# Second experts: the places of a tile's rows are copied into a small ring before the tile's results are sent

## The chip, the cores and the metric

The kernel runs on one core of a Trainium2 chip. The metric is the device time of one execution in microseconds (us), and the median over several runs is compared. The core has five engines that work side by side: TensorE (PE in the profile, its weight loads PEld), VectorE (DVE), ScalarE (ACT), GpSimd (POOL) and SyncE (SP), which here only starts transfers. The engines meet through semaphores.

## The reference

Two layers over x of 32 x 128 tokens with 128 channels. Each layer is an attention and then a mixture of experts, in which every token goes to 2 of 8 experts. The second mixture, which the change touches, is this for each chosen expert, and a shared expert on top for every token:

```
def _expert(x, w1, b1, w3, b3, w2, b2):
    h = jax.nn.silu((x @ w1 + b1) * (x @ w3 + b3))
    return h @ w2 + b2
...
biased = scores + gate_b
_, idx = lax.top_k(biased, K)
w = jnp.take_along_axis(scores, idx, axis=-1) * ROUTER_SCALE
```

D is 128, the hidden width 176, E is 8 and K is 2. The results of the two chosen experts are weighted by w and added.

## The kernel before, in words

Attention writes each token's row twice into a DRAM tensor `rows`, sorted by expert. A row has 132 numbers: the token's normed values, its place (column `IDX`, the row of `results` to which the expert's result belongs) and its weight (column `WGT`). The experts then work on tiles of 128 such rows. There are at most SLOTS = 71 tiles in a layer, and which expert a tile belongs to is read at run time from a map.

For a tile i of the second experts (`gated_experts`) the steps are:

- SyncE loads it into `xs`, slot i % 16 (`load`, L1884). XU = 16 slots form the ring.
- TensorE transposes it (`take`, L2045), ScalarE copies the transpose out (L1942), and TensorE multiplies by the expert's first weights (`widen`, L2059), which VectorE has copied from the resident weights (L1982).
- ScalarE and VectorE form the product and the SiLU (L1948, L1989, L1957), and TensorE multiplies by the second weights (`narrow`, L2078).
- VectorE scales the result by the rows' weights, read from `xs`, into `ys`, slot i % 8 (L2001). U = 8 slots form that ring, and VectorE waits until the send of tile i - 8 has landed.
- GpSimd sends the 128 result rows to their places in the DRAM tensor `results` by an indirect transfer (`send`, L1929). Before the change it reads the places straight from the tile in `xs`.

The tiles go in pairs: one unit of work holds two routed tiles or two rows of blocks for the shared expert. The list UNITS starts with 7 shared units, then come 36 routed ones with three shared ones between, and 6 shared ones stand at the end. Of a unit u, TensorE does the first product, then takes the tiles of unit u + 2, then does the second product of unit u - 2.

Since the places are in `xs`, a slot of `xs` may be loaded anew only when the send that reads it has landed. So `load(i)` for i of 16 and more waits for the transpose (L1880), the scaled result (L1881) and the landed send (L1882) of tile i - 16. SyncE handles all its transfers in program order. Behind the last of the 71 loads stands `combine`: SyncE waits until the first 55, then 63, then all 71 sends have landed (`results_stored`, L1893), and after each loads a piece of the combined results into `yg` (L1901, named first_w in the trace). These are added by VectorE or, for the last blocks, by TensorE (L2084), the blocks 28 to 31 last.

The first experts (`experts`) already have the form with a copied place: `note` (L1618) copies it on GpSimd to `xi` with 8 slots, `send` (L1625) reads it there. There the note of tile n + 1 stands before the send of tile n. `early` in the trace is the memory that holds `ys`.

Of the kernel before, what the change touches and what calls it, by code (L numbers as in the profile page):

```python
# [14 lines left out]
U32 = mybir.dt.uint32  # L15
ALU = mybir.AluOpType
# [19 lines left out]
SLOTS = 2 * N // 128 + E - 1  # L36
# [4 lines left out]
X0, IDX, WGT = 1, D + 1, D + 2  # L41
# [194 lines left out]
class Steps:  # L236
# [10 lines left out]
    def wait(self, eng):  # L247
        eng.wait_ge(self.sem, self.n)
# [6 lines left out]
def attention(nc, st, layer, w):  # L255
# [156 lines left out]
    def fill_up(eng, experts):  # L412


        eng.wait_ge(st["maps_ready"], layer + 1)
        for e in experts:
            count = 128 * (1 if e < E - 1 else 1 + PAST)
            first = nc.s_assert_within(eng.value_load(st["fill"][0:1, e:e + 1]), 0, (e + 1) * REGION - 128,
                                       skip_runtime_bounds_check_because="a region has room for all the tokens")
            eng.dma_start(rows[bass.ds(first, count), :], st["filling"][e * 128:e * 128 + count, :]).then_inc(filled, 16)  # L420
# [1114 lines left out]
def experts(nc, st, w, maps_set, early_set):  # L1535

    U = 8
    FC = 4
    ctx, sh = st["ctx"], st["shared"]

    def sem(name):
        return ctx.enter_context(nc.semaphore(f"{name}_e0"))
# [4 lines left out]
    xs, xi, xsT, ys, w1s = sh["xs"], sh["xi"], sh["xsT"], sh["ys"], sh["w1s"]  # L1547
# [3 lines left out]
    hTp, xTp, yp = banks[0:2], banks[2][:, 0, :], banks[3][:, 0, :]  # L1551

    xs_in = st["xs_in"]
    xi_copied = sem("xi_copied")
    xsT_ready, xsT_copied = sem("xsT_ready"), sem("xsT_copied")
    hT_ready, hT_copied = sem("hT_ready"), sem("hT_copied")
    yp_ready, ys_ready = sem("yp_ready"), sem("ys_ready")
    ys_out = st["ys_out"][0]
    w1_copied = st["w1_copied"] = sem("w1_copied")
    rows, results = w["rows"], w["results"]  # L1560
# [202 lines left out]
def gated_experts(nc, st, w, early_set, maps_set, x_updated, shared_turned):  # L1763
# [7 lines left out]
    U = 8  # L1771
    XU = 16
# [4 lines left out]
    ctx, sh = st["ctx"], st["shared"]  # L1777

    def sem(name):
        return ctx.enter_context(nc.semaphore(f"{name}_e1"))  # L1780
# [1 line left out]
    x, cst, emap, rowmap = st["x"], st["cst"], st["emap"], st["rowmap"]  # L1782
    ident = cst[:, C_ID:C_ID + 128]
    W1r, W1s, W2, bsh = st["W1r"], st["W1s"], w["W2"], st["bsh"]
    xs, ys, yg, xall = sh["xs"], sh["ys"], sh["yg"], st["xall"]
    xsT, cs, hm, hT, w1s = sh["xsT2"], sh["cs"], sh["hm"], sh["hT2"], sh["w1s2"]
    S, ptp = sh["S"], sh["ptp"]

# [3 lines left out]
    w1_copied = sem("w1_copied")  # L1792
    up_ready, cs_ready, hm_ready, hT_ready = sem("up_ready"), sem("cs_ready"), sem("hm_ready"), sem("hT_ready")
    yp_ready, ys_ready, z_ready = sem("yp_ready"), sem("ys_ready"), sem("z_ready")
    ys_out = st["ys_out"][1]
    results_in = [sem(f"results_in{c}") for c in range(4)] + [st["pairs_in"]]
    landed = [32] * 4 + [32 * (NP // 2) + 32]
    x_done, dve_step = sem("x_done"), sem("dve_step")
    rows, results = w["rows"], w["results"]
# [69 lines left out]
    def row_of(eng, i):  # L1869
        return nc.s_assert_within(eng.value_load(mapped(rowmap, i, EARLY)), 0, SHARED - 128,  # L1870
                                  skip_runtime_bounds_check_because="the map's rows are those of its experts' tiles")
# [4 lines left out]
    def load(sp, i, row=None):  # L1876

        s, before = i % XU, i - XU
        if i >= XU:
            sp.wait_ge(xsT_ready, before // 2 + 1)  # L1880
            sp.wait_ge(ys_ready, before + 1)  # L1881
            sp.wait_ge(ys_out[before % U], 16 * (before // U) + 16)  # L1882
        at = row_of(sp, i) if row is None else row
        sp.dma_start(xs[:, s, :], rows[bass.ds(at, 128), :]).then_inc(xs_in[s], 16)  # L1884

    def in_place(eng, i):

        eng.wait_ge(xs_in[i % XU], first_use[i % XU] + 16 * (i // XU) + 16)
# [32 lines left out]

    def gpsimd(pool):

        def send(i):

            s, place = i % U, xs[:, i % XU, IDX:IDX + 1].bitcast(U32)
            in_place(pool, i)
            pool.wait_ge(ys_ready, i + 1)
            nc.gpsimd.indirect_dma_start(results[:, :], bass.IndirectOffsetOnAxis(place, 0), ys[:, s, :], None).then_inc(ys_out[s], 16)  # L1929

        for i in range(SLOTS):
            send(i)

    def scalar(act):
# [101 lines left out]
    def tensor(pe):  # L2036
# [51 lines left out]
        for u in range(NU + 2):  # L2088
# [17 lines left out]
            yield u  # L2106

    return {"load": load, "first_row": first_row, "combine": combine, "gpsimd": gpsimd, "scalar": scalar,
            "vector": vector, "tensor": tensor}


def build(nc, dram):

    with ExitStack() as ctx:
# [67 lines left out]
        prefetch += [(st["W1r"][:, :, :], dram["e1_W1"]), (st["W1s"][:, :], dram["e1_sW1"]), (st["bsh"][:, :], dram["e1_sB"]),  # L2182
                     (w1["W2"][:, :, :, :], dram["e1_W2"])]
        for name in ("cst_in", "three_set", "consts_in", "ident_ready", "weights_in", "maps_ready", "x_out", "bias_in", "raw_in", "stats_ready",
                     "w1_less"):
            st[name] = ctx.enter_context(nc.semaphore(f"{name}_all"))
        st["xs_in"] = [ctx.enter_context(nc.semaphore(f"xs_in{s}_all")) for s in range(8)]
        st["lasts_in"] = [ctx.enter_context(nc.semaphore(f"lasts_in{i}_all")) for i in range(2)]
# [5 lines left out]
        results = [nc.dram_tensor(f"results{l}", (2 * N + (E + PAST) * 128, D), F32, kind="Internal").ap() for l in range(2)]  # L2194
# [3 lines left out]
        def later_loads(sp):  # L2198

            sp.dma_start(st["cst"][:, C_SOON:], dram["cst"][:, C_SOON:]).then_inc(st["consts_in"], 16)  # L2200
            for l in range(2):
# [7 lines left out]
        a0 = attention(nc, st, 0, {**{k: dram[f"a0_{k}"] for k in names + ("am", "amT", "pad", "padT")},  # L2209
                                   "rows": rows[0], "prefetch": prefetch, "last_weights": last_weights})  # L2210
        e0 = experts(nc, st, {**w0, "rows": rows[0], "results": results[0]}, a0["maps_set"], a0["early_set"])
        a1 = attention(nc, st, 1, {**{k: dram[f"a1_{k}"] for k in names}, "gb": dram["e1_gb"], "rows": rows[1],
                                   "results": results[0], "prefetch": []})
        e1 = gated_experts(nc, st, {**w1, "rows": rows[1], "results": results[1]}, a1["early_set"], a1["maps_set"], a1["x_updated"], a1["shared_turned"])

        def run(part):
# [175 lines left out]
```

## Time and profile before

| | |
|---|---|
| median of 3 runs | 696.37 us (694.57 to 697.83) |
| span of the profiled execution | 763.9 us |
| profiled span less the median | 67.5 us |
| TensorE busy | 671.5 us, 88% |
| VectorE busy | 523.5 us, 69% |
| GpSimd busy | 504.9 us, 66% |
| ScalarE busy | 415.8 us, 54% |

The rows of the trace come from one execution under the hardware profiler. Its span is longer than the runs that give the median. In a row of a timeline the first number is the start, the second how long the merged instructions last, and what stands in brackets is the idle time of the engine before them with what ended it. "issue" means that nothing in the profile ended it.

### The profile page before, as it was taken

To read this page: it belongs to the slowest core of one execution; us is meant where nothing else is said; L and a number is where in the kernel's file an instruction comes from. 1 tells how busy PE (TensorE), PEld (TensorE's weight loads), DVE (VectorE), ACT (ScalarE), POOL (GpSimd) and SP (SyncE) were. 2 spreads that over 40 slices of the span, in tenths; PEclk is the share of its full clock that TensorE was granted. 3 is DMA by queue.
4 is the path that set the end of the run, shared out by engine and by line. 5 is a ranking of instruction groups with operands and counts; after the bars stand their busy time and mean duration, and the time that the engine had idled before them with its cause. 6 is when DMAs were issued, how large, how long until landed. Compare 5 with 4: busy or idle time off the path is not lost.

```text
span 763.9 us, 21054 instructions
## 1 busy us (share of the span) xinstructions
PE 671.5 (88%) x7092; PEld 546.5 (72%) x7092; DVE 523.5 (69%) x1515; ACT 415.8 (54%) x1158; POOL 504.9 (66%) x837
## 2 busy tenths in 40 slices
PE   8799998888876999999979999888888668788797
PEld 7567666665646999999957776666667568778787
DVE  5489988888663446555358898888886555555556
ACT  5477767654542434444447777656547445555563
POOL 5975788577564678877677778777667635455451
PEclk9899999999997999999979999999989989899999
DMA  5470000001331522343110101111211312222264
GB/s 166 124 305 2 17 27 27 27 30 36 137 99 48 160 70 81 97 127 89 46 36 29 30 26 40 54 37 37 66 34 37 89 51 77 61 75 72 75 232 152
DMA packets 45406, 57.78 MB, mean 76 GB/s; under 512 B 11379, under 2 KB 37142, under 8 KB 44630
## 3 DMA queue, kind: packets, MB, share of 16 engines
q1 hardware_dynamic: 36086, 38.17, 16.6%
q0 software_dynamic: 8640, 17.97, 7.1%
q8 instruction: 60, 0.98, 0.5%
q10 hardware_dynamic: 576, 0.29, 0.1%
q14 instruction: 44, 0.36, 0.1%
HBM read 33.82 MB, written 22.08 MB: 73 GB/s over the span
## 4 chain that ended last, share of the span: by engine, by line
PE 50%; POOL 17%; issue 12%; DVE 8%; ACT 5%; another core or an unknown queue 4%; DMA 2%; SPq 1%; DVEq 0%; POOLq 0%; ACTq 0%
POOL results L1625 9%; PE ptp L1349 8%; PE M L1366 7%; PE ptp L2078 6%; PE S L1326 5%; PE S L2059 5%; PE S L1330 3%; PE ptp L1352 3%; POOL xi L1618 2%; POOL rows L626 2%; PE M L1374 2%; PE M L1418 2%; PE S L2065 1%; SPq L707 1%
## 5 line engine op out<-in xcount | busy, mean ns | idle before, releaser
L626 POOL DMA_INDIRECT rows<-out_rows,posi x128 | 126.9, 991 | 50.1 <-issue 32.1
L806 ACT ACTIVATE pT<-ptp 128x512 f32<-128x512 f32 (+1 forms) x192 | 95.1, 525 | 97.7 <-PE ptp L1349 87.0
L1929 POOL DMA_INDIRECT results<-early,xs x71 | 69.0, 971 | 68.4 <-DVE early L2001 50.9
L1064 DVE TENSOR_REDUCE mx<-S 128x16 f32<-128x1232 f32 x64 | 91.3, 1427 | 18.3 <-PE S L1330 16.4
L1625 POOL DMA_INDIRECT results<-early,xi x71 | 75.9, 1069 | 40.5 <-DVE early L1687 35.1
L1065 DVE TENSOR_TENSOR pr<-S,mx 128x1232 f32<-128x1232 f32 x64 | 92.3, 1442 | 2.2
L1724 PE MATMUL S<-first_w,early 128*128 x568 | 77.2, 279 | 3.0 <-DVE early L1687 1.5
L1714 PE MATMUL S<-early,w1s 128*128 128x128 f32 x568 | 76.9, 279 | 0.6 <-ACT early L1659 0.6
L1366 PE MATMUL M<-pT,vm 128*32 128x128 f32 (+1 forms) x2048 | 74.7, 283 | 1.1 <-ACT pT L806 0.6
L1349 PE MATMUL ptp<-cst,pr 128*128 128x128 f32 x512 | 74.0, 290 | 0.0
L1724 PEld LDWEIGHTS S<-first_w,early 128*128 128x128 f32 x568 | 69.5, 193 | 5.9 <-issue 5.7
L1687 DVE TENSOR_SCALAR early<-S,xs 128x128 f32<-128x128 f32 x71 | 24.9, 351 | 68.0 <-PE S L1724 39.2
L1714 PEld LDWEIGHTS S<-early,w1s 128*128 128x128 f32 x568 | 70.8, 196 | 0.9 <-ACT early L1659 0.9
L1349 PEld LDWEIGHTS ptp<-cst,pr 128*128 128x128 f32 x512 | 58.6, 147 | 16.1 <-issue 16.0
L1659 ACT ACTIVATE early<-S 128x128 f32<-128x128 f32 x71 | 19.7, 277 | 90.3 <-PE S L1707 51.7
L2078 PE MATMUL ptp<-W,kT 128*128 (+1 forms) x412 | 63.6, 301 | 5.4 <-ACT kT L1959 3.8
L1366 PEld LDWEIGHTS M<-pT,vm 128*32 128x32 f32 (+1 forms) x2048 | 52.5, 112 | 18.1 <-issue 13.8
L2078 PEld LDWEIGHTS ptp<-W,kT 128*128 128x128 f32 x412 | 57.4, 212 | 8.8 <-issue 7.8
L2059 PE MATMUL S<-early,w1s 128*128 128x128 f32 x426 | 60.2, 297 | 3.1 <-issue 1.3
L2059 PEld LDWEIGHTS S<-early,w1s 128*128 128x128 f32 x426 | 57.1, 213 | 4.1 <-issue 4.0
L1326 PE MATMUL S<-first_w,qT 32*128 32x308 f32 x512 | 52.5, 479 | 6.9 <-POOL first_w L569 2.8
L1989 DVE TENSOR_TENSOR pr<-S,pr 128x256 f32<-128x256 f32 (+1 forms) x72 | 26.7, 413 | 41.7 <-ACT pr L1948 24.4
(221 smaller groups left out, 1527.9 us busy)
## 6 DMA issues: line engine op xcount, KB each, us to landing
xs<-rows SPq DMA_DIRECT2D x142, 66.0 KB
first_w<-in_e_W SPq DMA_DIRECT2D x2, 2048.0 KB, 8.2
swap<-results SPq DMA_DIRECT2D x32, 128.0 KB
first_w<-results SPq DMA_DIRECT2D x6, 512.0 KB
rows<-out_rows,posi POOLq DMA_INDIRECT x128
x_res<-in_x SPq DMA_DIRECT2D x1, 1536.0 KB, 8.4
W1r<-in_e_W SPq DMA_DIRECT2D x1, 1536.0 KB, 10.8
out_x<-x_res SPq DMA_DIRECT2D x3, 512.0 KB, 2.7
```

The lines of the kernel that those rows point to most:

```text
L626: nc.gpsimd.indirect_dma_start(rows[:, :], bass.IndirectOffsetOnAxis(posi[:, k, n:n + 1], 0), out_rows[:, ring_slot(groups, n), k, :], Non ...
L806: nc.scalar.activation(pT[0:rows_of, G * r:G * r + count, :], ptp[q % 2][0:rows_of, 0:count, :], ACT.Exp, scale=SCALE)\
L1064: do(V.tensor_reduce(mx[:, :].rearrange("p (g j) -> p g j", g=G), sc, AX.X, ALU.max))
L1065: V.tensor_tensor(pr[:, n % 2, :, :].rearrange("p (g j) k -> p g j k", g=G), sc, mx[:, :].rearrange("p (g j) -> p g j", g=G).unsqueeze(3). ...
L1326: nc.tensor.matmul(S[:, g, 0:GK], qT[heads, n % 2, :], kexp[heads, n % KR, :, :], start=True, stop=True, skip_group_check=True)
L1349: last = nc.tensor.transpose(ptp[q % 2][:, g, :], flat[:, g // 2, at:at + 128], ident)
L1366: last = nc.tensor.matmul(OT[32 * g:32 * g + 32, half * T:(half + 1) * T], vm[0:rows_of, n % 2, block + g, :], pT[0:rows_of, chunk, :], st ...
L1625: nc.gpsimd.indirect_dma_start(results[:, :], bass.IndirectOffsetOnAxis(xi[:, s:s + 1], 0), ys[:, s, :], None)\
L1714: last = nc.tensor.matmul(hTp[n % 2][:, c, :], w1s[:, n % 3, c * 128:(c + 1) * 128], xsT[:, n % 3, :], start=True, stop=True)
L1724: last = nc.tensor.matmul(yp, hT[:, n % 2, c, :], w2[:, c, :], start=(c == 0), stop=(c == FC - 1))
L2059: last = nc.tensor.matmul(out[:, at * 128:(at + 1) * 128], w1s[:, u % 2, at, c * 128:(c + 1) * 128], xsT[:, r % 3, at, :], start=True, sto ...
L2078: last = nc.tensor.matmul(yp(u)[:, at, :], hT[:, u % 2, c * 256 + at * 128:c * 256 + (at + 1) * 128], w2[:, c, :], start=(c == 0), stop=(c ...
```

## The change

The second experts get a `note` of their own. It copies the places of tile i to `xi`, slot i % 8, right before the send of tile i, and the send reads them there. The load of tile i then waits for the copied place of tile i - 16 in the place of its landed send. The semaphore `xi_copied` is shared by both layers, so the second starts its count at SLOTS.

```
-            sp.wait_ge(ys_out[before % U], 16 * (before // U) + 16)
+            sp.wait_ge(xi_copied, SLOTS + before + 1)
...
     def gpsimd(pool):
 
+        def note(i):
+
+            s = i % U
+            wait(pool, ys_out[s], 16 * (i // U))
+            in_place(pool, i)
+            nc.gpsimd.tensor_tensor(xi[:, s:s + 1], xs[:, i % XU, IDX:IDX + 1].bitcast(U32), st["zero"][:, 0:1], ALU.add).then_inc(xi_copied, 1)
+
         def send(i):
 
-            s, place = i % U, xs[:, i % XU, IDX:IDX + 1].bitcast(U32)
-            in_place(pool, i)
+            s = i % U
             pool.wait_ge(ys_ready, i + 1)
-            nc.gpsimd.indirect_dma_start(results[:, :], bass.IndirectOffsetOnAxis(place, 0), ys[:, s, :], None).then_inc(ys_out[s], 16)
+            pool.wait_ge(xi_copied, SLOTS + i + 1)
+            nc.gpsimd.indirect_dma_start(results[:, :], bass.IndirectOffsetOnAxis(xi[:, s:s + 1], 0), ys[:, s, :], None)\
+                .then_inc(ys_out[s], 16)
 
         for i in range(SLOTS):
+            note(i)
             send(i)
```

## Rows read from the trace of the kernel before

**Rows 1.** Busy time by stage, from 580 us on (time, then busy us and count).

```profile
core 0: us, PE busy (x) PEld busy (x) DVE busy (x) ACT busy (x) POOL busy (x), PEclk, DMA share, GB/s
...
580.00:764.00 184.00, 148.07 (x1064) 138.28 (x1064) 107.57 (x345) 95.25 (x248) 90.34 (x97) 0.92 0.30 94
```

**Rows 2.** The chain of waits, 712 to 726 us (start, us, what).

```profile
714.85 1.34 PE S L2059 x12
...
722.21 2.02 PE S L2059 x12
```

**Rows 3.** Waits of TensorE, 612 to 764 us (total, times, longest).

```profile
PE M L2045 <- ACT early L1942: 13.9, 7, 4.6
...
PE M L2045 <- issue: 3.6, 3, 2.0
```

**Rows 4.** Waits of GpSimd, 612 to 764 us.

```profile
POOL results L1929 <- DVE early L2001: 50.9, 20, 8.3
POOL results L1929 <- issue: 17.4, 51, 1.0
```

**Rows 5.** Timeline of GpSimd, 739 to 749 us.

```profile
740.32 0.96 POOL L1929 DMA_INDIRECT results<-early,xs  x1 [2.17 <-DVE early L2001]
741.58 0.96 POOL L1929 DMA_INDIRECT results<-early,xs  x1 [0.30 <-issue]
...
747.94 0.96 POOL L1929 DMA_INDIRECT results<-early,xs  x1 [0.30 <-issue]
```

**Rows 6.** The line of the sends (duration in ns, first and last start).

```profile
L1929 POOL DMA_INDIRECT results<-early,xs x71: 956/962/1217, 619.9 to 747.9; - x71
```

**Rows 7.** Timeline of SyncE's loads, 622 to 689.6 us, and the last alone.

```profile
622.68 66.81 SPq L1884 DMA_DIRECT2D xs<-rows  x36
...
689.15 0.33 SPq L1884 DMA_DIRECT2D xs<-rows  x1
```

**Rows 8.** Timeline of SyncE, 749.5 to 751.5 us.

```profile
750.34 0.80 SPq L1901 DMA_DIRECT2D first_w<-results  x2
```

**Rows 9.** Timeline of VectorE, the last scaled result.

```profile
744.60 0.33 DVE L2001 TENSOR_SCALAR early<-ptp,xs 128x128 f32<-128x128 f32 x1
```

**Rows 10.** The line of TensorE's takings up to 695.3 us.

```profile
L2045 PE MATMUL M<-cst,xs x52: 272/273/475, 600.8 to 695.2; 128*128 128x128 f32 x52
```

**Rows 11.** Transfers by issue (KB each, median us to landing).

```profile
out_x<-x_res SPq DMA_DIRECT2D x2, 256.0 KB, 2.7
...
bv<-in_a_bv ACTq DMA_DIRECT2D x1, 64.0 KB, 3.7
```

**Rows 12.** Waits of SyncE, 618 to 764 us.

```profile
SPq L1893 <- DMA results<-early,xs: 11.6, 3, 9.8
SPq L1882 <- DMA results<-early,xs: 8.0, 15, 1.7
```

**Rows 13.** Timeline of GpSimd in the first experts, 353 to 358 us.

```profile
353.47 1.05 POOL L1625 DMA_INDIRECT results<-early,xi  x1 [0.45 <-DVE early L1687]
354.55 0.20 POOL L1618 TENSOR_TENSOR xi<-xs,zero 128x1 uint32<-128x1 uint32 x1
354.91 1.22 POOL L1625 DMA_INDIRECT results<-early,xi  x1 [0.16 <-POOL xi L1618]
...
356.52 0.99 POOL L1625 DMA_INDIRECT results<-early,xi  x1 [0.16 <-POOL xi L1618]
```

**Rows 14.** Timelines of GpSimd and VectorE in the first experts, 309 us.

```profile
309.11 0.44 POOL L1618 TENSOR_TENSOR xi<-xs,zero 128x1 uint32<-128x1 uint32 x1
...
309.09 0.42 DVE L1680 COPY w1s<-first_w 128x512 f32 x1
```

**Rows 15.** Timeline of TensorE, 756.3 to 760 us.

```profile
757.08 0.61 PE L2084 MATMUL ptp<-first_w,cst 128*128 128x128 f32 x4
```

**Rows 16.** Timeline of ScalarE, 742 to 751 us.

```profile
750.42 0.42 ACT L1957 ACTIVATE kT<-pr 128x256 f32<-128x256 f32 x1 [3.40 <-remote]
```

More of the change, by code:

```diff
@@ L1553, in experts @@
     xs_in = st["xs_in"]
-    xi_copied = sem("xi_copied")
+    xi_copied = st["xi_copied"]
     xsT_ready, xsT_copied = sem("xsT_ready"), sem("xsT_copied")
@@ L1784, in gated_experts @@
     W1r, W1s, W2, bsh = st["W1r"], st["W1s"], w["W2"], st["bsh"]
-    xs, ys, yg, xall = sh["xs"], sh["ys"], sh["yg"], st["xall"]
+    xs, ys, xi, yg, xall = sh["xs"], sh["ys"], sh["xi"], sh["yg"], st["xall"]
     xsT, cs, hm, hT, w1s = sh["xsT2"], sh["cs"], sh["hm"], sh["hT2"], sh["w1s2"]
@@ L1794, in gated_experts @@
     yp_ready, ys_ready, z_ready = sem("yp_ready"), sem("ys_ready"), sem("z_ready")
-    ys_out = st["ys_out"][1]
+    ys_out, xi_copied = st["ys_out"][1], st["xi_copied"]
     results_in = [sem(f"results_in{c}") for c in range(4)] + [st["pairs_in"]]
@@ L2184, in build @@
         for name in ("cst_in", "three_set", "consts_in", "ident_ready", "weights_in", "maps_ready", "x_out", "bias_in", "raw_in", "stats_ready",
-                     "w1_less"):
+                     "w1_less", "xi_copied"):
             st[name] = ctx.enter_context(nc.semaphore(f"{name}_all"))
```

## The prediction

> **What bounds the kernel now.** I read the busy times by stage first. From 580 us to the end, the stage the change touches, TensorE works 148.07 of 184.00 us and GpSimd 90.34 [rows 1]. So TensorE carries the stage and GpSimd is second. The chain of waits says how the carrier walks. In an undisturbed stretch the products of one pair of tiles start at 714.85 us and those three pairs on at 722.21 [rows 2]: 7.36 / 3 = 2.45 us a pair, with nothing but TensorE's lines between. That is TensorE's pace, two tiles each 2.45 us.
>
> Next I asked who waits for whom. The longest wait of TensorE's taking of a tile (L2045) is for ScalarE's copy, 13.9 us in all, and the next, 3.6 us, waits for nothing the profile shows [rows 3]. Not one wait of TensorE is for a landed load. GpSimd waits for a result of VectorE in 20 cases, 50.9 us; in the other 51 it has its next tile already and only pays its own gap [rows 4].
>
> GpSimd's own pace comes from its timeline. Where results are ready, sends start at 740.32, 741.58, ... 747.94, seven of them: 7.62 / 6 = 1.27 us a tile, 0.96 of work and 0.30 of gap [rows 5]. A pair costs 2.54 us, already slightly more than TensorE's 2.45. It keeps up because TensorE is often slower: the 71 sends lie between 619.9 and 747.9 us [rows 6], so about 129 us with the last one's work, and need 71 x 1.27 = 90.
>
> **The change, part by part.** *1. The loads move forward.* Now the load of tile i waits for the send of tile i - 16 to land; afterwards for VectorE's result of i - 16 and for its copied place, which GpSimd takes before it waits for that result. The first such load leaves at 622.68 us [rows 7]; the send that it waits for started at 619.9 [rows 6], and that send's result was ready a little earlier. A send needs 2.40 us until SyncE passes the wait on it (the last starts at 747.94 [rows 5], the load behind it leaves at 750.34 [rows 8]), and before that a result waits for GpSimd: the last one is ready at 744.60 + 0.33 and sent at 747.94, 3.0 us later [rows 5, 9], and in the middle it is 0.8 to 2 us. So a load can leave about 3 us earlier. What is that worth? The 36th load of this series (tile 51) leaves at 689.15 [rows 7]; the 52nd taking starts at 695.2 [rows 10]: a lead of 6.0 us, the shortest of the 55 that I worked out in this way; most are 8 to 11. Loads of 66 KB have no landing time on the page; the nearest rows are 3.7 us for 64 KB and 2.7 us for 256 KB [rows 11]. Even at 3.7 us the shortest lead leaves 2.3 us. A load that comes earlier ends no wait of TensorE: worth 0. What hides it is the ring of 16 tiles. SyncE itself waits 8.0 us in 15 cases for landed results before loads [rows 12]; that wait goes, and SyncE then stands at the wait for the result instead. Behind the last load stand the loads of the combined results, whose own wait (11.6 us in 3 cases [rows 12]) needs the same sends to land as before, so they do not move forward either.
>
> *2. A copy is added before each send: 71.* The first experts run this same pair, so their rows price it. Back to back, sends start at 353.47, 354.91 and 356.52, with a copy of 0.20 between [rows 13]: 1.44 and 1.61 us a tile against 1.27. The parts: send 0.99 to 1.22, gap 0.02, copy 0.20, gap 0.16. Bounds: 0.96 + 0.02 + 0.20 + 0.16 = 1.34 from below; from above 1.22 + 0.02 + 0.44 + 0.16 = 1.84, with the copy of 0.44 us found at 309.11 [rows 14]. I take 1.50, between the two whole rounds seen, nearer the lower end because in the second experts the sends take 0.96 almost always by the median of [rows 6]. That adds 0.23 us a tile, 71 x 0.23 = 16.3 us of GpSimd.
>
> Does it lie on the path? Total first: 71 x 1.50 = 106.5 us in a stretch of 129: it fits. If the runs without a profile are shorter everywhere by the same share (696.37 / 763.9 = 0.912), the stretch is 117.5 us: still fits. Locally: in a fast stretch a pair costs GpSimd 3.00 us against TensorE's 2.45, so its lag grows by 0.55 a pair. VectorE needs the place of a result free 8 tiles, that is four pairs or 9.8 us, later; less 2.4 us of landing it bears a lag of 7.4. The lag now peaks near those 3.0 us, so some eight pairs at full pace without a break would be needed, and in the trace the pace breaks sooner: the fourth pair of the stretch of [rows 2] already takes 2.02 instead of 1.34 us for its products. Each send that has to wait for VectorE hides one copy wholly, since the copy stands before that wait. Worth 0 in the middle.
>
> A rule bears on the price of the copy. The row first: the copy of a place took 0.44 us at 309.11 where VectorE copied weights from 309.09 to 309.51, and 0.20 where it did not [rows 13, 14]. The Trainium skill, "SBUF — State Buffer", section "Who interferes with whom", says that a GpSimd instruction and a VectorE copy in a two-port mode exclude each other for the whole instruction, and whoever starts second waits. The trace agrees for these copies. By that rule a note that meets a weight copy costs 0.24 us more; the sum above goes by the rows.
>
> *3. The end.* Sends 64 to 70 run back to back [rows 5]. Six more rounds at +0.23 put the last at 749.3 instead of 747.94, and the last load of combined results at 751.7 instead of 750.34 [rows 8]. Its blocks, 28 on, are first read by TensorE at 757.08 [rows 15]: with the 2.7 us of the 256 KB row it has landed by 754.4, with 3.7 by 755.4. It fits, with 1.7 us or more to spare. But in between all engines stand (ScalarE 3.40 us until 750.42, by a releaser the profile cannot name [rows 16]). If the runs without a profile lack that stop, the slack before the change is -0.3 to 0.7 us, and the 1.4 us that the change adds cost 0.7 to 1.4. So the end costs 0 to 1.4 us, by whether that stop is there; I take 0.6.
>
> *4. The shared semaphore* counts on past the first experts' 71. It adds no wait that is not met: 0.
>
> **Sum.** Against the profiled execution: 763.9 + 0 + 0 + 0.6 = 764.5. The runs shown have a median of 696.37, 67.5 us below that span. The trace does not say where all of that lies; stops like the one in [rows 16] are a candidate. I carry the difference over unchanged: 696.37 + 0.6 = 697.0.
>
> **Rivals.** *A, GpSimd becomes the bound (slower).* The place is the 71 sends. Its point of decision: 117.5 / 71 = 1.65 us a tile. If copies meet VectorE's weight copies as at 309.11, a round is 1.50 + 0.24 = 1.74, and 71 x 1.74 = 123.5 us, 6 more than there is; with the longer lag at the end, 6 x 0.47 = 2.8 less the slack, the time is 702 to 705. For it: pairs already run at 2.54 against 2.45, and GpSimd's lag is used up fastest just where TensorE is best. Against it: only 1.44 and 1.61 were seen back to back in quiet rows, and 20 idle spells hold 50.9 us. Chance 0.17. Two or three points more go to smaller losses at the end that pass 0.5%.
>
> *B, the loads did bind (faster).* Without profiling TensorE may run closer to 2.45 us a pair throughout, and leads shrink. The ring of 16 turns 55 / 16 = 3.4 times; each turn would gain 3.2 us, less the 2.3 us of slack now seen, if that slack is truly the limit: 0.9 x 3.4 = 3; with the slack gone, 3.4 x 3.2 = 11. Time 685 to 693. For it: the profiled execution is the slower one. Against it: no wait of TensorE for a load, and slack even at 3.7 us of landing. Chance 0.13.
>
> *C, the change does not do what it says.* The copy stands behind the previous send, so if GpSimd lags, the place is copied late and the load moves less than 3 us. Nothing hangs on the move, so the time is that of my forecast, 696 to 698. It shares the chance of the forecast, together 0.68.
>
> **Numbers.** Forecast 697.0; alone it ranges from 694 to 699.5 (end cost 0 to 1.4, and the spread 694.57 to 697.83 of the runs). I stretch to 692.5, taking in the mild half of B, and to 702, where A begins. About 0.5%, 3.5 us, is what a measurement of this kernel can tell from no change. Faster by more: 0.13 (B). Within: 0.68. Slower by more: 0.19 (A and the bad ends).
>
> **What would show it.** Right: 71 new GpSimd copies of about 0.2 us; rounds of 1.44 to 1.6 us back to back; GpSimd's busy time up by 14 us or more in a stage of equal length; the first reused load leaves near 620 and leads grow by about 3 us; SyncE's 8.0 us for landed results before loads gone; still no wait of TensorE for loads. Wrong for A: VectorE's results (L2001) waiting for landed sends, sends back to back throughout, copies of 0.4 us. Wrong for B: shorter pairs in the middle, with the stretch from first to last send clearly under 129 us.

## The result, and the profile after

The change makes the kernel slower: 746.89 us (744.01 to 748.75, 4 runs) against 696.13 us (694.57 to 697.83, 4 runs), ratio 1.0711 with the 95% interval 1.0675 to 1.0748. That is 50.8 us more, against a forecast of 0.6. The profiled execution took 745.3 us with a span of 743.5, so this profile shows what the timed runs do.

Its head and its chain of waits, by engine and then by line:

```profile
span 743.5 us, 21188 instructions
...
POOL 31%; PE 24%; DVE 20%; issue 17%; DMA 4%; ACT 2%; SPq 2%; POOLq 1%; DVEq 0%; ACTq 0%
POOL results L1625 10%; POOL results L1936 7%; DVE mx L1064 5%; POOL rows L626 5%; DVE pr L1065 4%; PE ptp L1349 3%; PE M L1366 3%; PE S L1326 3%; POOL xi L1618 2%; PE ptp L2087 2%; POOL xi L1929 2%; POOL rstd L554 2%; PE S L2068 2%; PE S L1330 2%; SPq L707 1%
```

The second experts' sends and copies (now L1936 and L1929) are among the chain's lines. The line of the sends, which answers to [rows 6]:

```profile
L1936 POOL DMA_INDIRECT results<-early,xi x71: 982/985/1378, 585.2 to 728.4; - x71
...
  POOL xi L1929: 42.3, 55
...
  DVE early L2010: 13.3, 14
```

The 71 sends take 143.2 us from the first start to the last. In 55 of 71 cases the row names GpSimd's own copy as what ended the idle time. The 14 cases that name VectorE must be read with care: only the first send really waited for it. From the second send on, each send starts at least 2.40 us after its own result has ended, and the gap is 0.76 us there as well, so there too the copy was the last thing to be waited for. A stretch of GpSimd's timeline, which answers to [rows 5]:

```profile
601.50 0.98 POOL L1936 DMA_INDIRECT results<-early,xi  x1 [0.76 <-POOL xi L1929]
602.51 0.20 POOL L1929 TENSOR_TENSOR xi<-xs,zero 128x1 uint32<-128x1 uint32 x1
603.47 0.98 POOL L1936 DMA_INDIRECT results<-early,xi  x1 [0.76 <-POOL xi L1929]
604.48 0.20 POOL L1929 TENSOR_TENSOR xi<-xs,zero 128x1 uint32<-128x1 uint32 x1
605.44 0.98 POOL L1936 DMA_INDIRECT results<-early,xi  x1 [0.76 <-POOL xi L1929]
```

A round is 603.47 - 601.50 = 1.97 us: 0.98 of send, 0.03, 0.20 of copy, and 0.76 from the copy's end to the send's start. The reader should see that the copy is the small part and the gap behind it the large one. The first experts have 0.16 in that place [rows 13].

The waits of all engines, which show how the late sends pass back:

```profile
POOL results L1936 <- POOL xi L1929: 42.3, 55, 0.9
...
DVE early L2010 <- DMA results<-early,xi: 20.6, 14, 3.5
...
PE ptp L2093 <- DMA first_w<-results: 9.7, 1, 9.7
...
PE M L2054 <- DMA xs<-rows: 7.7, 12, 2.0
```

VectorE waits 20.6 us for places of the result ring to be sent. TensorE now does wait for loads, 7.7 us, since a load waits for a copy that stands behind the late sends in GpSimd's order. At the end it waits 9.7 us for the combined results. TensorE is not what carries the stage any more, although its granted clock is lower there (0.95; the kernel before has 1.00 in its second profile below): it is busy 119.78 of 147 us, in this row of the busy times by stage.

```profile
582.00:729.00 147.00, 119.78 (x879) 109.71 (x877) 86.06 (x242) 77.15 (x203) 87.09 (x143) 0.95 0.29 84
```

The waits from SyncE's side, to be held against [rows 12]:

```profile
SPq L1882 <- POOL xi L1929: 59.4, 52, 2.2
SPq L1893 <- DMA results<-early,xi: 30.7, 7, 12.2
```

So the change made the loads wait more, not less: 59.4 us for a copied place, against 8.0 us for landed sends in [rows 12] and 23.5 us in the second profile of the kernel before.

### The profile page after: what moved, and what is told of

Same layout as the page of the kernel before. It is cut to its first block, busy times and chain, and to the rows that moved or that the text cites. A ratio compares the mean times of both kernels' runs of the same rounds, so it can differ in the third digit from the quotient of the medians.

```text
span 743.5 us, 21188 instructions
## 1 busy us (share of the span) xinstructions
PE 661.2 (89%) x7092; PEld 541.9 (73%) x7092; DVE 524.1 (70%) x1515; ACT 417.7 (56%) x1158; POOL 522.9 (70%) x908
## 4 chain that ended last, share of the span: by engine, by line
POOL 31%; PE 24%; DVE 20%; issue 17%; DMA 4%; ACT 2%; SPq 2%; POOLq 1%; DVEq 0%; ACTq 0%
POOL results L1625 10%; POOL results L1936 7%; DVE mx L1064 5%; POOL rows L626 5%; DVE pr L1065 4%; PE ptp L1349 3%; PE M L1366 3%; PE S L1326 3%; POOL xi L1618 2%; PE ptp L2087 2%; POOL xi L1929 2%; POOL rstd L554 2%; PE S L2068 2%; PE S L1330 2%; SPq L707 1%
## 5 line engine op out<-in xcount | busy, mean ns | idle before, releaser
L1936 POOL DMA_INDIRECT results<-early,xi x71 | 70.9, 999 | 57.7 <-POOL xi L1929 42.3
L1625 POOL DMA_INDIRECT results<-early,xi x71 | 76.3, 1075 | 33.4 <-DVE early L1687 27.4
L1714 PE MATMUL S<-early,w1s 128*128 128x128 f32 x568 | 76.6, 279 | 0.8 <-ACT early L1659 0.8
L1349 PE MATMUL ptp<-cst,pr 128*128 128x128 f32 x512 | 72.6, 286 | 0.5 <-ACT kT L678 0.3
L1714 PEld LDWEIGHTS S<-early,w1s 128*128 128x128 f32 x568 | 70.6, 195 | 0.9 <-ACT early L1659 0.9
L1366 PE MATMUL M<-pT,vm 128*32 128x128 f32 (+1 forms) x2048 | 70.0, 277 | 0.0
L1349 PEld LDWEIGHTS ptp<-cst,pr 128*128 128x128 f32 x512 | 57.0, 144 | 16.8 <-issue 15.8
L2068 PE MATMUL S<-early,w1s 128*128 128x128 f32 x426 | 56.9, 285 | 6.9 <-DVE w1s L1991 6.5
L2068 PEld LDWEIGHTS S<-early,w1s 128*128 128x128 f32 x426 | 53.1, 200 | 8.6 <-issue 8.5
L2010 DVE TENSOR_SCALAR early<-ptp,xs 128x128 f32<-128x128 f32 x71 | 22.6, 344 | 39.0 <-DMA results<-early,xi 20.6
## 6 DMA issues: line engine op xcount, KB each, us to landing
swap<-results SPq DMA_DIRECT2D x32, 128.0 KB
```

Source lines behind the costliest of these rows:

```text
L1349: last = nc.tensor.transpose(ptp[q % 2][:, g, :], flat[:, g // 2, at:at + 128], ident)
L1366: last = nc.tensor.matmul(OT[32 * g:32 * g + 32, half * T:(half + 1) * T], vm[0:rows_of, n % 2, block + g, :], pT[0:rows_of, chunk, :], st ...
L1714: last = nc.tensor.matmul(hTp[n % 2][:, c, :], w1s[:, n % 3, c * 128:(c + 1) * 128], xsT[:, n % 3, :], start=True, stop=True)
L2068: last = nc.tensor.matmul(out[:, at * 128:(at + 1) * 128], w1s[:, u % 2, at, c * 128:(c + 1) * 128], xsT[:, r % 3, at, :], start=True, sto ...
```

## The experiments

The kernel before was timed again with each group of runs (medians 695.91 and 696.64 us), and each ratio is against the runs of its group. The last four runs below belong to the second group.

**The kernel before, once more.** Its code is unchanged. What I expected:

> The kernel before, profiled once more, because its first profile was 67.5 us longer than its timed runs while the profile of the changed kernel agrees with its own (743.5 against 745.3). Theory A (the first profile was slowed by something that the timed runs lack, and hid how tight GpSimd is): a span near 694 us, the second experts' sends within 90 to 100 us in place of 128, most of them back to back at 1.27 us, almost no rounds ended by a longer idle. Theory B (the profile is typical, the change found time elsewhere): a span near 760 again and sends over 120 us or more.

Measured: 695.13 us (8 runs), ratio 0.9997 (0.9972 to 1.0022), span 691.3. Its line of sends, its timeline of GpSimd, TensorE's only wait in this stage, SyncE's wait before loads, and the busy times by stage:

```profile
L1929 POOL DMA_INDIRECT results<-early,xs x71: 954/958/1112, 583.3 to 676.7; - x71
```

```profile
592.27 0.96 POOL L1929 DMA_INDIRECT results<-early,xs  x1 [0.30 <-issue]
593.53 0.96 POOL L1929 DMA_INDIRECT results<-early,xs  x1 [0.30 <-issue]
594.80 0.96 POOL L1929 DMA_INDIRECT results<-early,xs  x1 [0.30 <-DVE early L2001]
```

```profile
PE S L2059 <- DVE w1s L1982: 1.4, 1, 1.4
```

```profile
SPq L1882 <- DMA results<-early,xs: 23.5, 29, 2.9
```

```profile
580.00:677.00 97.00, 95.61 (x817) 94.13 (x816) 77.15 (x226) 71.56 (x192) 68.55 (x71) 1.00 0.42 126
```

The sends take 93.4 us, not the 128.0 of [rows 6]. The usual round is 1.265 us (two of them from 592.27 to 594.80), and 70 of these would be 88.6, so GpSimd has at most 4.8 us to spare in the whole stage and runs nearly without a break, beside a TensorE that is busy 95.61 of 97 us. The stops with a releaser the profile cannot name, as in [rows 16], are not there. This is what theory A said. The profile on which the prediction rests was of an execution much slower than the timed ones, and the 35 us by which its sends were spread out were taken for room.

**The copy one tile ahead.** The changed kernel, but tile i + 1 is copied before tile i is sent:

```
+        note(0)
         for i in range(SLOTS):
-            note(i)
+            if i + 1 < SLOTS:
+                note(i + 1)
             send(i)
```

> The changed kernel, with the place of tile i + 1 copied before the send of tile i, so the copy that a send waits for is one send old. Theory A (a send that waits for its own copy exposes the 0.76 us from the met wait to the start of the send, which otherwise runs under the work before): rounds of 0.98 + 0.03 + 0.20 + 0.16 = 1.37 to 1.5 us in place of 1.97, so 71 x (1.37 to 1.5 less 1.27) = 7 to 16 us over the kernel before, 703 to 713 us. Theory B (the copy itself is what costs, as work of GpSimd or by its port): no change, 740 to 750 us. Theory C (the earlier loads are in the way of the sends): 740 to 750 us too.

Measured: 704.96 us, ratio 1.0123 (1.0087 to 1.0159).

```profile
600.96 0.99 POOL L1936 DMA_INDIRECT results<-early,xi  x1 [0.16 <-POOL xi L1929]
601.97 0.20 POOL L1929 TENSOR_TENSOR xi<-xs,zero 128x1 uint32<-128x1 uint32 x1
602.33 0.99 POOL L1936 DMA_INDIRECT results<-early,xi  x1 [0.16 <-DVE early L2012]
```

The gap behind the copy is 0.16 again, a round 1.37, and 41.9 of the 50.8 us are back. The copies, loads and sends are the same; only the order differs.

**A copy that nobody reads.** The kernel before with this added ahead of a send; `unread_xi` is a tile of its own, and loads and places are as before:

```
+            nc.gpsimd.tensor_tensor(sh["unread_xi"][:, i:i + 1], st["zero"][:, 0:1], st["zero"][:, 1:2], ALU.add)
             pool.wait_ge(ys_ready, i + 1)
```

> The kernel before, with a copy of the same size on GpSimd before each send that nobody reads or waits for; loads and the source of the places as before. It computes the reference. Theory A: rounds of 1.37 to 1.5 us, 703 to 713 us. Theory B: 740 to 750 us. Theory C: no change, 696 us, but for the copy's own 0.2 us.

Measured: 701.97 us, ratio 1.0078 (1.0047 to 1.0109), a little under the range of theory A.

```profile
603.88 0.99 POOL L1930 DMA_INDIRECT results<-early,xs  x1 [0.16 <-issue]
604.90 0.20 POOL L1928 TENSOR_TENSOR unread_xi<-zero 128x1 uint32<-128x1 uint32 x1
605.25 0.99 POOL L1930 DMA_INDIRECT results<-early,xs  x1 [0.16 <-issue]
```

The copy costs 5 to 6 us by itself (3 to 8 by the interval), without any moved load. One thing more differs here: the wait for VectorE's result, an instruction of its own ahead of each send in the kernel before, is now carried by the send. What that is worth alone was not run.

**The same copy, waited for.**

```
+            ... ALU.add).then_inc(unread_set, 1)
             pool.wait_ge(ys_ready, i + 1)
+            pool.wait_ge(unread_set, SLOTS + i + 1)
```

> The same unread copy, but the send waits for it by a semaphore; loads and the source of the places as in the kernel before. Theory A: rounds of 1.97 us and the whole loss, 740 to 750 us. Theory B: the same as without the wait. Theory C: 696 to 713 us, since the loads have not moved.

Measured: 746.0 us, ratio 1.0699 (1.0662 to 1.0736): the whole loss of the change, with the source of the places and the condition of each load as before it. The difference of 44 us to the run above comes from one semaphore, which the copy raises and the next send waits for.

```profile
603.52 0.98 POOL L1933 DMA_INDIRECT results<-early,xs  x1 [0.76 <-POOL unread_xi L1930]
604.54 0.20 POOL L1930 TENSOR_TENSOR unread_xi<-zero 128x1 uint32<-128x1 uint32 x1
605.50 0.98 POOL L1933 DMA_INDIRECT results<-early,xs  x1 [0.76 <-POOL unread_xi L1930]
```

Theories B and C fall: the copy as work costs 5 to 6 us, and the loss is there without the moved loads. In the trace the wait for the copy is an instruction of its own ahead of each of the 71 sends:

```profile
L1932 POOLq EVENT_SEMAPHORE  x71: 17/17/17, 582.9 to 727.6; - x71
```

**Half of the waits.** As above, with the wait only where i is even.

> The unread copy for every tile, waited for by the sends of the even tiles alone. Theory A (each wait on the engine's own last copy costs 0.6 us of a round, by itself): rounds of 1.38 and 1.97 us in turn, 702 + 35.5 x 0.6 = 723 us, give or take 4. Rival (the waits break a flow once and for all, so half of them cost as much as all): 740 us or more; or the slack of the other rounds takes them up: under 712 us.

Measured: 724.09 us, ratio 1.0389 (1.0361 to 1.0416).

```profile
601.62 0.98 POOL L1934 DMA_INDIRECT results<-early,xs  x1 [0.16 <-DVE early L2006]
602.63 0.20 POOL L1930 TENSOR_TENSOR unread_xi<-zero 128x1 uint32<-128x1 uint32 x1
603.59 0.98 POOL L1934 DMA_INDIRECT results<-early,xs  x1 [0.76 <-DVE early L2006]
```

The gaps are 0.76 and 0.16 in turn. Each wait costs by itself, and half of them half as much: 22 of 44 us. Every copy raises the semaphore here too, so it is the wait that costs and not the raising.

**One and a half copies.** The unread, unwaited copy and a second one for every other tile.

> The unread and unwaited copy of the earlier run, and a second one for every other tile. The first copy costs only 0.11 us because it fills part of the 0.30 us gap that two sends have between them anyway; the second has no gap left. Theory A: 35.5 x 0.2 = 7 us more than the 702.0 of one copy, 707 to 711 us. Theory B (copies are hidden, and the loss of 6 us had another source): 702 us.

Measured: 708.45 us, ratio 1.0178 (1.0141 to 1.0215), 6.5 us over the single copy for 36 more copies: 0.18 us each, against 0.085 for the first (6.06 / 71, from 701.97 - 695.91). The two runs belong to different groups, whose medians of the kernel before are 0.7 us apart, so this 0.18 may be 0.16. The first copy lies in part in the 0.30 us that two sends have between them anyway:

```profile
602.15 0.20 POOL L1928 TENSOR_TENSOR unread_xi<-zero 128x1 uint32<-128x1 uint32 x1
602.30 0.20 POOL L1930 TENSOR_TENSOR unread_xi<-zero 128x1 uint32<-128x1 uint32 x1
602.65 0.98 POOL L1932 DMA_INDIRECT results<-early,xs  x1 [0.16 <-DVE early L2004]
```

**One copy for two tiles, a pair ahead.** `note` copies 128 x 2 places, and is called for i + 2 before the send of each even i.

> The changed kernel with one copy on GpSimd for the places of two tiles, a pair ahead of its sends. Theory A: half of the 0.11 us that a copy adds to a round when it stands ahead, 71 x 0.055 = 4 us over the kernel before, so about 700 us, between before and the copy ahead for every tile (705). Theory B (a copy costs by something other than the round, such as a late load): no difference from 705.

Measured: 697.14 us, ratio 1.0008 (0.9991 to 1.0025). That is cheaper than the 4 us that theory A gave.

```profile
602.61 0.98 POOL L1937 DMA_INDIRECT results<-early,xi  x1 [0.16 <-POOL xi L1930]
603.89 0.96 POOL L1937 DMA_INDIRECT results<-early,xi  x1 [0.31 <-DMA results<-early,xi]
604.88 0.20 POOL L1930 TENSOR_TENSOR xi<-xs,zero 128x2 uint32<-128x2 uint32 x1
605.24 0.98 POOL L1937 DMA_INDIRECT results<-early,xi  x1 [0.16 <-POOL xi L1930]
```

The average round is near 1.32 us, which would add 70 x 0.05 = 3.5 us, and the sends lie within 95.2 us, 1.8 more than before. So the room of up to 4.8 us seems to take up most of it; no run took that apart.

**The copy on VectorE.** The changed kernel without GpSimd's copy. VectorE makes it, before it scales the tile's result:

```
+                    V.tensor_tensor(xi[:, i % U:i % U + 1], xs[:, i % XU, IDX:IDX + 1].bitcast(U32), st["zero"][:, 0:1], ALU.add).then_inc(xi_copied, 1)
                     V.tensor_scalar(ys[:, i % U, :], yp(u)[:, at, :], xs[:, i % XU, WGT:WGT + 1], None, ALU.mult).then_inc(ys_ready, 1)
```

> The changed kernel with the copy of the place on VectorE, right before it scales the tile's result; GpSimd only sends, and the loads wait for the copied place as in the change. This is the moved load without its price on GpSimd. Theory A (GpSimd's rounds set the pace, the earlier load is worth nothing): rounds of 1.27 us again, leads of the loads 3 us longer than the 4.95 (median) of the kernel before, and the time within 0.4% of it, 694 to 699 us, with up to 3 us of loss where VectorE's 71 extra operations delay a result. Theory B (the loads were close to binding, shortest lead 2.7 us against 1.9 of landing): 5 us faster or more.

Measured: 697.53 us (12 runs), ratio 1.0024 (1.0004 to 1.0044). This is the moved load without a copy on GpSimd; VectorE has 71 copies of about 0.15 us more. GpSimd is back at its old pace:

```profile
601.63 0.96 POOL L1929 DMA_INDIRECT results<-early,xi  x1 [0.30 <-issue]
602.89 0.96 POOL L1929 DMA_INDIRECT results<-early,xi  x1 [0.30 <-DVE early L2003]
```

SyncE's waits before loads are for VectorE now, no longer for landed sends:

```profile
SPq L1882 <- DVE early L2003: 22.8, 23, 3.5
...
SPq L1882 <- DVE xi L2002: 1.0, 3, 0.4
```

From the starts of loads and takings, worked out as in the prediction, the median lead grows from 4.95 us (kernel before, second profile) to 9.1 and the shortest from 2.7 to 6.5. The time does not fall. The earlier load is had, and is worth nothing: in the second profile of the kernel before TensorE waits for no load of this stage, so there is nothing to win. No version that I ran beats the kernel before.

## Why the prediction was wrong

*The step that failed first: the gap of the copy's round.* The prediction put a round together as 0.96 + 0.02 + 0.20 + 0.16 and took 1.50 us; it measured 1.97. The 0.16 came from rows of the first experts [rows 13], where the copy of tile n + 1 stands before the send of tile n, so a send's own copy is one send old and the wait on it is met long before. In the change the copy stands right ahead of the send that waits for it. There the row that fits is another, which the prediction used only as a delay of results ("in the middle it is 0.8 to 2 us"). In the kernel before, a result that GpSimd stands idle for is sent 0.76 us after its end: the first of these two results ends at 622.48 + 0.33 = 622.81, and its send starts at 623.57.

```profile
622.48 0.59 DVE L2001 TENSOR_SCALAR early<-ptp,xs 128x128 f32<-128x128 f32 x2
...
623.57 0.96 POOL L1929 DMA_INDIRECT results<-early,xs  x1 [1.43 <-DVE early L2001]
```

There too the wait is an instruction of its own ahead of the send (71 of them at L1928). The 0.76 us belong to such a wait, not to every late wait. In the change only the wait for the copy is of that kind, and the send carries the wait for VectorE's result itself. At the first send, where the copy was long done and the result late, the gap is 0.28 us: the result started at 584.54, took 0.333 and so ended at 584.88.

```profile
585.16 1.38 POOL L1936 DMA_INDIRECT results<-early,xi  x1 [2.27 <-DVE early L2010]
```

Part 4 of the prediction has the same error in words. It says that the semaphore of the copies "adds no wait that is not met" and puts it at 0, but the send's wait on that semaphore stands right behind the copy that raises it, and was open each time: 0.60 us more a round than the 0.16 that the sum had. Even the bound from above, 1.84, was too low, since it lengthened send and copy and left the gap alone.

*The second: the room.* "71 x 1.50 = 106.5 us in a stretch of 129: it fits." The stretch is 93.4 us in an execution as long as the timed ones. The prediction saw that the profile was 67.5 us longer than the median and carried the difference over unchanged, or at best in proportion (117.5 us). By the second profile, which is 72.6 us shorter than the first, they were mostly this: the second experts' first result at 582.2 us in place of 618.8, and 34.6 us less between first and last send. Rival A had the right path, GpSimd as the bound, but not the cause: it took the copies to be longer and left the gap alone. Its point of decision, 1.65 us a round, should have been 93.4 / 70 = 1.33.

*The sum with both terms as measured:* 70 rounds at 1.97 are 137.9 us. The sends took 143.2; the other 5.3 are rounds that were longer than the usual 1.97. Less the 93.4 of before that is 49.8 us, of the 50.8 measured. Between the two profiles, 743.5 and 691.3 us long, the rest is 1.9 us by which the first send starts later and 0.5 us at the end.

*"Each send that has to wait for VectorE hides one copy wholly".* In the profile after, only the first send waited for VectorE; every later result was at least 2.40 us old when it was sent. So there was hardly any such cover.

*The end.* The prediction put it at 0 to 1.4 us: six rounds at +0.23, less what slack there is. From the last send's start to the end of the span it is 15.1 us after and 14.6 before, so no slack hid any of the last send's delay, which is the prediction's case without the stop of [rows 16]. But the delay was that of all 71 sends, and six rounds alone at +0.70 are 4.2 us, so the size was wrong with the round.

*Right: the moved load is worth nothing.* The copy on VectorE shows it. But the landing time needed no bound: the profiles after give 1.8 to 1.9 us. And the shortest lead of the kernel before is 2.7 us, not 6.0, so the slack was 0.8 us and not 2.3 or more. *Rival C*, a load that moves less because its copy stands behind late sends, is what happened (59.4 us of SyncE's waits; worked out in the same way, the median lead fell from 4.95 to 3.35 us), and it made TensorE wait 7.7 us. With the waited but unread copy the loads wait for landed sends as before the change. There the median lead is 2.97 us, TensorE waits 11.1 us for loads, and the time is the same within 1 us. So the new condition of the loads did not add to the loss: where GpSimd sets the pace, TensorE's waits for loads only take the place of others.

*The price of a copy beside VectorE.* Rival A had 0.44 us for each copy, from [rows 14]. In the run after, the copies have a median of 0.197 us and a longest of 0.664. Nine of the 71 took over 0.25 us; all that the copies took over their median is 1.9 us together. So a copy held up beside VectorE is rare here, and it was not the cause. The rule itself stands: the Trainium skill, "SBUF — State Buffer", section "Who interferes with whom", says that a GpSimd instruction which starts while VectorE copies in a two-port mode is blocked until that copy is over. The trace agrees for five of the nine, which started inside a weight copy of VectorE and ended 0.04 us after it (one ran from 660.50 to 660.84 beside a copy that ended at 660.80). The other four stood beside VectorE's additions.

The runs together fall on a line once the usual round is over about 1.3 us:

| usual round of GpSimd, us | time, us |
|---|---|
| 1.27 (before) | 696 |
| 1.27 (copy on VectorE) | 697.5 |
| 1.32, mean of 1.28 and 1.35 (one copy for two) | 697.1 |
| 1.37 (copy one ahead) | 705.0 |
| 1.38 (unread copy) | 702.0 |
| 1.44, mean of 1.37 and 1.51 (three copies for two sends) | 708.5 |
| 1.67, mean of 1.37 and 1.97 (half of the waits) | 724.1 |
| 1.97 (unread copy waited for) | 746.0 |
| 1.97 (the change) | 746.9 |

From 1.38 to 1.97 it is 44.0 us for 0.59 us: 75 us for each us of round, close to the 71 tiles. Above about 1.3 us GpSimd sets the pace.

Open: whether the copy one ahead is really slower than the unread copy with the same round. The medians are 3 us apart, but its seven times go from 699.5 to 709.0 us and take in the 702.0, and no run took it apart. Open too is what slowed the first profiled execution of the kernel before. The stops that name "remote" stand in that profile alone, 20.5 us in 6 cases on the line of ScalarE that has most of them, and its granted clock was 0.953 against 0.980 in the second.

## What to carry to other kernels

Price an added operation by a row that has the same order and the same wait, not only the same instructions: the copy was 0.20 us, the wait of the very next send on it 0.60 us more. If an instruction waits for another of the same engine that stands right before it, put one other piece of work between them. And when a profile is clearly longer than the timed runs, take the slack it shows out of the sum: the distance of two starts in a stretch where an engine works back to back gives the pace that it does not beat (here 1.27 us a tile, 2.54 a pair; busy time divided by the count would give 0.97, since it leaves the gap out), and the question is whether the others, undisturbed, reach it (TensorE's 2.45 us a pair did).

## What the runs showed of the hardware

An indirect send on GpSimd starts 0.76 us after the end of the copy just before it if it waits for that copy, and 0.16 us after a copy for which it does not wait. Between two sends without a late wait the gap is 0.30 us, and a copy of 128 x 1 placed there costs 0.09 to 0.11 us (0.085 by the times, 0.11 by the rounds) in place of its 0.20. A late result of VectorE is followed by its send after 0.76 us in the kernel before, where the wait for it is an instruction of its own, and after 0.28 us at the first send of the change, where the send carries that wait. That fits a send whose preparation, 0.5 to 0.6 us by these gaps (0.76 less 0.28 or 0.16, an estimate), runs under the instruction before it, unless a wait instruction ahead of the send holds it back. The traces show the gaps, not the preparation itself.
